# Projecting the next pair's K, Q and values inside the last norm of the pair before

## The reference, cut to what matters

```python
h = _L0_tok_ref(x, ...)                              # token mixing
h = _layernorm(h + _L0_attn_ref(h, ...), axis=-1)    # selective scan, norm 0
h = _layernorm(h + _L0_ffn_ref(h, ...), axis=-1)     # 16 experts, top 2, norm 1
h = _layernorm(h + _L1_attn_ref(h, ...), axis=-1)    # windowed attention, norm 2
h = _layernorm(h + _L1_ffn_ref(h, ...), axis=-1)     # routed two-layer FFN, norm 3

def _L0_tok_ref(x, d_gamma, Wq, bq, Wk, bk, Wv, bv, Wo, bo, prelu_a):
    q = x @ Wq + bq;  k = x @ Wk + bk;  v = x @ Wv + bv
    scores = jnp.einsum('btd,bsd->bts', q, k)
    retained = jnp.einsum('bts,bsd->btd', d_gamma * scores, v)
    y = retained @ Wo + bo
    return jnp.where(y >= 0, y, prelu_a * y)

def _layernorm(x, axis=-1, eps=1e-05):
    m = jnp.mean(x, axis=axis, keepdims=True);  v = jnp.var(x, axis=axis, keepdims=True)
    return (x - m) / jnp.sqrt(v + eps)
```

## Time and profile before

| | |
|---|---|
| median of three runs | 1545.95 us (1545.62 to 1551.45) |
| the profiled execution's own time | 1543.89 us |
| its span, first to last instruction | 1542.1 us |
| TensorE busy | 1319.3 us, 86% |
| VectorE busy | 1057.0 us, 69% |
| ScalarE busy | 603.4 us, 39% |
| GpSimd busy | 461.8 us, 30% |
| mean granted TensorE clock | 0.946 of full speed |

### The profile page before, as it was taken

How to read it: one execution, slowest core, us unless ns; L and a number is a source line. 1 busy time by engine, 2 the same in 40 slices (tenths; PEclk the granted TensorE clock), 3 DMA queues, 4 the chain that set the end, 5 groups by cost and what they waited for, 6 DMA issues and landing times. The chain is left out here.

```text
span 1542.1 us, 16298 instructions
## 1 busy us (share of the span) xinstructions
PE 1319.3 (86%) x5546; PEld 562.1 (36%) x5546; DVE 1057.0 (69%) x1218; ACT 603.4 (39%) x887; POOL 461.8 (30%) x262
## 2 busy tenths in 40 slices
PE   6957789988986789999897778999989686999897
PEld 2312333346422233325632323332663232333265
DVE  2599955674559995567456998656736599755673
ACT  0344343344254435325425343432441634343334
POOL 3268800022007970002100896000300189400030
PEclk9979999998997999999898799999989889999997
DMA  8334420000013432000001342200000234210000
GB/s 245 102 126 150 149 63 7 1 1 1 14 44 118 148 131 69 1 0 1 1 14 58 123 164 96 69 1 1 1 1 14 71 134 164 81 46 0 1 1 14
DMA packets 43378, 93.63 MB, mean 61 GB/s; under 512 B 6786, under 2 KB 23970, under 8 KB 42786
## 3 DMA queue, kind: packets, MB, share of 16 engines
q1 hardware_dynamic: 42690, 88.25, 17.6%
q10 hardware_dynamic: 608, 4.34, 0.9%
HBM read 87.84 MB, written 4.73 MB: 60 GB/s over the span
## 5 line engine op out<-in xcount | busy, mean ns | idle before, releaser
L443 POOL TENSOR_TENSOR scratch<-scratch 128x1024 f32<-128x1024 f32 x124 | 297.4, 2414 | 354.5 <-DVE scratch L1138 353.5
L593 PE MATMUL ps<-scratch,consts 128*128 128x512 f32 x512 | 257.3, 637 | 6.2 <-POOL scratch L443 6.2
L457 POOL TENSOR_TENSOR work<-work,rmax 128x512 f32<-128x512 f32 x64 | 67.4, 1053 | 621.8 <-DVE rmax L1285 621.8
L1138 DVE TENSOR_TENSOR_SCAN scratch<-ps,scratch 128x1024 f32<-128x1024 f32 x100 | 225.5, 2278 | 0.5
L911 ACT ACTIVATE ps<-steps,vec 128x1024 f32<-128x1024 f32 x128 | 143.0, 1117 | 208.9 <-DVE scratch L1138 206.8
L1187 DVE TENSOR_TENSOR scratch<-scratch,ps 128x1024 f32<-128x1024 f32 x108 | 131.9, 1221 | 118.2 <-PE ps L654 114.4
L571 PE MATMUL ps<-bc,pick 128*128 128x512 bf16 x256 | 83.9, 412 | 141.5 <-DVE scratch L1127 104.3
L957 ACT ACTIVATE scratch<-ps 128x1024 f32<-128x1024 f32 x108 | 108.8, 1022 | 175.6 <-PE ps L641 175.6
L593 PEld LDWEIGHTS ps<-scratch,consts 128*128 128x128 f32 x512 | 104.3, 206 | 125.9 <-issue 99.0
L641 PE MATMUL ps<-h_odd,w 64*128 64x512 f32 x512 | 140.9, 636 | 3.8 <-ACT scratch L957 3.8
L654 PE MATMUL ps<-scratch,w 64*128 64x512 f32 x512 | 134.9, 602 | 8.5 <-DVE scratch L1187 8.5
(11 more groups left out here) (197 smaller groups left out, 1666.2 us busy)
## 6 DMA issues: line engine op xcount, KB each, us to landing
scratch<-c_rows SPq DMA_DIRECT2D x128, 512.0 KB, 3.8
steps<-routed_table SPq DMA_DIRECT2D x128, 64.5 KB, 1.9
decayT<-in_decayT SPq DMA_DIRECT2D x8, 512.0 KB, 16.5
work<-in_table ACTq DMA_DIRECT2D x1, 2064.0 KB, 13.8
routed_table<-work SPq DMA_DIRECT2D x1, 2064.0 KB, 6.4
w<-in_w ACTq DMA_DIRECT2D x4, 512.0 KB, 20.9
out<-h_even SPq DMA_DIRECT2D x4, 512.0 KB, 2.6
bc<-in_x_next SPq DMA_DIRECT2D x3, 512.0 KB, 3.6
```

The costliest lines, as they stand in the source:

```text
L443: pool.tensor_tensor(hc_slot(k), hs_slot(k), c_slot(k), ALU.mult).then_inc(sem["hc_ready"], 1)
L593: m = mm(ps[:, 6 + c, :], ident, hc_slot(k)[:, c * CH:(c + 1) * CH], start=(n == 0), stop=(n == NS - 1))
L1138: dve.tensor_tensor_scan(hs_slot(k), banks(dA_bank(k)), dbu_slot(k), 0.0, ALU.mult, ALU.add).then_inc(sem["scanned"], 1)
```

## The change

TensorE projects K and Q of the next pair, a half at a time, inside norm 3: half 0 between the two halves of the output projection, half 1 between the variances of chunks 1 and 2. The values come behind the last variance. VectorE copies half 0 of K and Q in front of its first product, half 1 between products 1 and 2, and the values behind the last product; the Q copies go from ScalarE to VectorE. The values use banks 2 and 3, K's, after K is copied. Norm 3's variances use banks 6 and 7 twice, so the third and the fourth wait for the `rstd` of the first and the second. Scores of unit 1 now wait for the values' copies, and scores of unit 2 for `pair_done`. The first pair does the same projections in front of its own units.

```diff
-        VAR_BANKS = ((2, 3, 4, 5), (0, 1, 6, 7), (0, 1, 2, 3), (6, 7, 2, 3))
+        VAR_BANKS = ((2, 3, 4, 5), (0, 1, 6, 7), (0, 1, 2, 3), (6, 7, 6, 7))
...
@@ TensorE
+            def mix_kq(pair, c):
+                pe.wait_ge(sem["x_loaded"], at(pair, "x_loaded", 16))
+                if pair:
+                    pe.wait_ge(sem["l1_first"], at(pair - 1, "l1_first", c + 1))
+                    pe.wait_ge(sem["l1_second"], at(pair - 1, "l1_second", c + 1))
+                pe.matmul(ps[:, 2 + c, :], wk_bd[:, :], xT[:, c * CH:(c + 1) * CH], start=True, stop=True)\
+                    .then_inc(sem["k_ps"], 1)
+                pe.matmul(ps[:, c, :], wq_bd[:, :], xT[:, c * CH:(c + 1) * CH], start=True, stop=True)\
+                    .then_inc(sem["q_ps"], 1)
+
+            def mix_values(pair):
+                pe.wait_ge(fold_sb, 1)
+                pe.wait_ge(sem["k_tok_sb"], at(pair, "k_tok_sb", NC))
+                for t in range(NT):
+                    m = pe.matmul(ps[:, 2 + t // 4, (t % 4) * P:(t % 4 + 1) * P], xT[:, t * P:(t + 1) * P],
+                                  wvo_bd[:, :], start=True, stop=True)
+                    if t % 4 == 3:
+                        m.then_inc(sem["vw_ps"], 1)
...
                     for c in chunks:
+                        if k == 3 and c >= 2:
+                            pe.wait_ge(sem["rstd"], at(pair, "rstd", NN * k + c - 1))
                         pe.wait_ge(sem["squared"], at(pair, "squared", NN * k + c + 1))
...
-                pe.wait_ge(sem["x_loaded"], at(pair, "x_loaded", 16))
-                for c in range(NC):
-                    mm(ps[:, c, :], wq_bd[:, :], xT[:, c * CH:(c + 1) * CH], start=True, stop=True)\
-                        .then_inc(sem["q_ps"], 1)
-                pe.wait_ge(pair_done, pair + 1)
-                for c in range(NC):
-                    mm(ps[:, 2 + c, :], wk_bd[:, :], xT[:, c * CH:(c + 1) * CH], start=True, stop=True)\
-                        .then_inc(sem["k_ps"], 1)
-                pe.wait_ge(fold_sb, 1)
-                for t in range(NT):
-                    m = mm(ps[:, 6 + t // 4, (t % 4) * P:(t % 4 + 1) * P], xT[:, t * P:(t + 1) * P], wvo_bd[:, :],
-                           start=True, stop=True)
...
+                if pair == 0:
+                    for c in range(NC):
+                        mix_kq(0, c)
+                    mix_values(0)
...
+                    if n == 1:
+                        pe.wait_ge(sem["vw_sb"], at(pair, "vw_sb", 2))
                     if n == 2:
-                        pe.wait_ge(sem["vw_sb"], at(pair, "vw_sb", 2))
+                        pe.wait_ge(pair_done, pair + 1)
...
                     m.then_inc(sem["r_ready"], 1)
-                norm(3)
+                    if c == 0 and pair + 1 < PAIRS:
+                        mix_kq(pair + 1, 0)
+                norm(3, range(NN // NC))
+                if pair + 1 < PAIRS:
+                    mix_kq(pair + 1, 1)
+                norm(3, range(NN // NC, NN))
+                if pair + 1 < PAIRS:
+                    mix_values(pair + 1)
...
@@ ScalarE
-                for c in range(NC):
-                    act.wait_ge(sem["q_ps"], at(pair, "q_ps", c + 1))
-                    act.activation(q_tok[:, c * CH:(c + 1) * CH], ps[:, c, :], ACT.Identity, bias=v("bq"))\
-                       .then_inc(sem["q_sb"], 1)
...
@@ VectorE
+            def mix_kq(pair, c):
+                if pair:
+                    dve.wait_ge(sem["l1_first"], at(pair - 1, "l1_first", NC))
+                cols = slice(c * CH, (c + 1) * CH)
+                dve.wait_ge(sem["k_ps"], at(pair, "k_ps", c + 1))
+                dve.tensor_scalar(k_tok[:, cols], ps[:, 2 + c, :], v("bk"), None, ALU.add).then_inc(sem["k_tok_sb"], 1)
+                dve.wait_ge(sem["q_ps"], at(pair, "q_ps", c + 1))
+                dve.tensor_scalar(q_tok[:, cols], ps[:, c, :], v("bq"), None, ALU.add).then_inc(sem["q_sb"], 1)
...
-                norm(3)
+                if pair + 1 < PAIRS:
+                    mix_kq(pair + 1, 0)
+                norm(3, range(NN // NC))
+                if pair + 1 < PAIRS:
+                    mix_kq(pair + 1, 1)
+                norm(3, range(NN // NC, NN))
+                if pair + 1 < PAIRS:
+                    mix_values(pair + 1)
                 dve.memset(m1[:, :], 0.0).then_inc(pair_done, 1)
```

More of the change, by code:

```diff
@@ L482, in norm @@
                             .then_inc(sem["var_ps"], 1)
-                pe.wait_ge(sem["x_loaded"], at(pair, "x_loaded", 16))
-                for c in range(NC):
-                    mm(ps[:, c, :], wq_bd[:, :], xT[:, c * CH:(c + 1) * CH], start=True, stop=True)\
-                        .then_inc(sem["q_ps"], 1)
-                pe.wait_ge(pair_done, pair + 1)
-                for c in range(NC):
-                    mm(ps[:, 2 + c, :], wk_bd[:, :], xT[:, c * CH:(c + 1) * CH], start=True, stop=True)\
-                        .then_inc(sem["k_ps"], 1)
-                pe.wait_ge(fold_sb, 1)
-                for t in range(NT):
-                    m = mm(ps[:, 6 + t // 4, (t % 4) * P:(t % 4 + 1) * P], xT[:, t * P:(t + 1) * P], wvo_bd[:, :],
-                           start=True, stop=True)
-                    if t % 4 == 3:
-                        m.then_inc(sem["vw_ps"], 1)
+                if pair == 0:
+                    for c in range(NC):
+                        mix_kq(0, c)
+                    mix_values(0)
                 def scores(n):
@@ L519, in _ @@
                         scores(n + 2)
+                    if n == 0:
+                        pe.wait_ge(pair_done, pair + 1)
                     pe.wait_ge(sem["masked"], at(pair, "masked", n + 1))
@@ L1037, in _, with mix_values @@
             dve.tensor_scalar(skip[:, :], ident, v("D"), None, ALU.mult).then_inc(skip_ready, 1)
+            def mix_kq(pair, c):
[6 more added lines that the diff above has]
+                dve.tensor_scalar(q_tok[:, cols], ps[:, c, :], v("bq"), None, ALU.add).then_inc(sem["q_sb"], 1)
+            def mix_values(pair):
+                for c in range(2):
+                    dve.wait_ge(sem["vw_ps"], at(pair, "vw_ps", c + 1))
+                    dve.tensor_tensor(vw[:, 4 * c:4 * c + 4, :], ps[:, 2 + c, :].rearrange("p (a b) -> p a b", a=4),
+                                      vo_row[:, :].unsqueeze(1).to_broadcast([P, 4, P]), ALU.add)\
+                       .then_inc(sem["vw_sb"], 1)
             for pair in range(PAIRS):
```

## The result

The changed kernel is slower: 1557.4 us median (1555.95 to 1560.78) against 1547.3 (1545.62 to 1551.45) for the kernel before in the same comparison, ratio 1.0064 with a 95% interval of 1.0037 to 1.0092, about 10 us. That is 0.4 us above the upper end of the predicted range, and above the bound of 0.5% inside which it was forecast.

The account below looks back on a forecast made before the run. TensorE was taken to bound each boundary, with 0.60 us to win. Three boundaries (3.75) plus the last norm (1.8) added 5.55 us to the median 1545.95, giving 1551.5; range 1546 to 1557, the forecast's own 1548 to 1553.5.

Parts of the forecast that it names:

- What bounds a boundary, TensorE with 0.60 us to win: Between pairs, TensorE was said to set the length, busy 9.28 of 9.88 us, with 0.60 us idle to win.
- The chain through the norm: From foT through norm 3 to the next pair's retained matmul: each boundary 1.25 us longer, bounds 0.8 to 1.7.
- The wait on `rstd`, put together as 0.78: Norm 3's third and fourth variances: an Ln starts 0.78 us after an Exp has ended, bounds 0.51 and 1.2.
- First half of K and Q: Between the two foT halves: its matmuls gain nothing by themselves and delay the norm by 1.81 us.
- Q on VectorE: Q's copies at the boundary, moved from ScalarE to VectorE: no cost forecast for the move alone.
- the start of pair 0: K before Q in the first pair: costed at nothing, covered by the fifth mask's 3.35 us wait for the decay transfer.
- The clock in the boundary: TensorE's granted clock between pairs was forecast to stay 1.00 through the new idle of about 1.15 and 0.83 us.
- the third rival: At boundaries the clock falls to half rate, losing some 6 us each: 1569.5, or 1560 if back sooner; chance 0.07.
- The base: Whole kernel before: a median of 1545.95 us, to which the forecast's sum was added.
- the sum of 5.55: Whole kernel: 3.75 us for three boundaries plus 1.8 for the last pair's norm, other parts costed at nothing.
- From there TensorE is busy without a gap to 438, so nothing gives the loss back: Behind the first retained matmul after a boundary: TensorE has no gap, so the boundary's 1.25 us loss stays.
- The second rival: Slow engine hand-offs, 0.31 us each, in the boundary chain: 2.75 a boundary, 2.6 at the end, 1557; chance 0.14.

Follow-up runs that it names:

- e4: Kernel before, with K of the next pair waiting for the third rstd of the last norm instead of `pair_done`; 1555.93 us, 1.0045.
- e10: Kernel before with only norm 3's banks (6, 7, 6, 7) and the two rstd waits, nothing projected early; 1.0073.
- e11: Changed kernel with the first half of K and Q moved behind variances 0 and 1, in front of the second half; 1.0057 to the kernel before.
- e12: Kernel before with only Q's two copies moved from ScalarE to VectorE, each behind K's copy of the same half; 0.9977.
- e2: Kernel before with two chained VectorE memsets in front of the one that raises `pair_done`, delaying K at each boundary; 1560.84 us, 1.0093.
- e3: Kernel before with four chained VectorE memsets in front of the one that raises `pair_done`; 1574.85 us, 1.0177.
- e1: The changed kernel run once more, unaltered; 1556.57 us, 1.0071 to the kernel before.
- e5: Kernel before with two more 512-column matmuls between K and the values of pairs 1 to 3; 1.0052.
- e8: Kernel before with one more 512-column matmul between K and the values of pairs 1 to 3; 1.0020.
- e6: Kernel before with four more 512-column matmuls between K and the values of pairs 1 to 3; 1.0064.
- e13: Kernel before with six idle-filling matmuls per pair in the tail of the attention; 1543.11 us, 0.9963.

## Why the prediction was wrong

*What bounds a boundary, TensorE with 0.60 us to win:* right. e4 takes that wait away and gets 0.86: the 0.60, and 0.26 of TensorE's busy time (12.05 to 11.79).

*The chain through the norm:* right in each link, and off by a little. The third square came 4.05 after L826 started (forecast 3.79), Ln 2 at 7.25 (6.99), product 1 at 8.06 (7.82), the values at 9.35 (9.10), the scores at 11.30 (10.98), the first mask at 12.55 (12.23), the retained matmul at 14.17 (13.75 to 14.1). The 0.25 that all carry was lost in front of the third square: I gave the joints between foT, K and Q no time of their own. TensorE's two stops were shorter than forecast (0.87 and 0.57 for 1.15 and 0.83), but its busy time, for which the chain had no term, grew by 0.68. A boundary cost 1.52 where I took 1.25 (bounds 0.8 to 1.7).

*The wait on `rstd`, put together as 0.78:* Exp 0 of the last pair ends at 1551.87 and Ln 2 starts at 1552.66, 0.79. Ln 3 is 6.21 after foT, as worked out, and the end grew by 1.76 (1.8). e10 confirms the same price at a boundary.

*First half of K and Q, "they delay the norm by 1.81":* the squares moved, but it is not what the boundary paid for; e11 puts it at 0.36.

*Q on VectorE, the start of pair 0:* Q 0.26 in e12, forecast nothing alone. At the start the values came 0.06 earlier (18.04 before, 17.98 after) and the first mask 0.02 later, so nothing was lost there by the order; but the start itself varies by 3 us from one execution to another (58.05 to 61.34 in the table, in no order of the kernels).

*The clock in the boundary:* right, 1.00, and the third rival did not come true there. e2 and e3 show how far it was away: behind a wait of 4.35 us the next two matmuls ran at half rate in e3, behind three equal waits of 2.48 in e2 only the last time (3.54, and 1.98 twice). The Trainium skill (TensorE: Matmul & The Clock Gate, section "HAM oscillation — how this bites in real kernels") says that idle gaps between bursts send the array to half rate, and the next burst pays. The row of K in e3 agrees with it, and e2's rows agree in one of three.

*The base:* the kernel before came out at 1547.3 beside the change and not at 1545.95, so 1.35 of the 5.9 us between forecast and measurement is no part of the change. On the forecast's own base the measured 10.1 would have given 1556.1, inside the range; on which side of the range's end the time fell is luck. The other 4.5 are what the sum lacks.

*The step that failed* is the sum of 5.55. It counts three boundaries and an end, and puts the stages between, some 337 us a pair from the first convolution matmul to foT, at nothing. The sentence that stands for it, "From there TensorE is busy without a gap to 438, so nothing gives the loss back", holds for the 29 us that it names (29.61 from the retained matmul to the convolution in pairs 1 to 3 of every trace) and says nothing of what follows. The local part measures 6.3 and would have been in the range. What the sum lacks is in the pairs: 7.5 us more in the first trace of the change and 6.4 in e1's, by two long pairs of 340.5 in each, which stand against none among the last three pairs in both traces of the kernel before. A long pair differs from a short one by VectorE's product beside GpSimd's (2.75 for 0.67) and by where the low-clock stretches lie. The earlier trace rows shows the low clock behind the attention, and I read it as a property of a place. The single stretches in the scan, which I did not look at, move when a boundary moves. That long pairs are no mark of this change, e4, e5 and e8 show: shorter or longer boundaries, with no early projection at all, have them too.

The second rival named 1557, the time that came, but not by its mechanism: the hand-offs are not slow (0.79 for the trip), and a boundary cost 1.52 and not 2.75.

*What stays open.* Which shift brings long pairs and which doesn't: none of the runs gives a rule, and the one I tried (e6) failed. No run changed the order of VectorE's product and L451 alone, so what the product costs by itself is read from traces and not tested, and why it takes 2.75 beside L451 no run shows. The 6.3 us are shown to be the change's, by place and size, in every trace of it. How much of the rest is the change's isn't shown: half of the kernel before's own times are above 1551, none of those executions was traced, and beside the later medians of 1550.6 to 1551.8 the change was not run again (6.3 over them would be 1557 to 1558, about where it was measured). The interval of the first measurement (6 to 14 us) would hold 6.3 alone, that of e1 (7 to 15) just not.

## What to carry to other kernels

Before moving work into an idle engine's gap, ask which engine sets the length of that stretch: here TensorE was busy 9.28 of 9.88 us, so the best outcome was 0.6 us, and PSUM banks saved at the price of two return trips through another engine cost three times that. Where the clock of TensorE changes level in the stages behind, or an operation's length depends on what another engine does beside it, a shift of a microsecond can cost or give several there, so judge a change of under 1% by the stretches of both traces, boundary by boundary, and not by the total alone, and trace a long execution of the kernel before as well as a short one. And a stage whose matmuls are small and wait for each other may be worth filling: six idle matmuls a pair won 0.4%, and with a shorter boundary 1.2%.

## What the runs showed of the hardware that was not expected

Removing 0.86 us from each of three boundaries made a kernel 7 us slower (e4), and the same removal on top of e13 made it 9 to 13 us faster. From the first convolution to foT the same instructions took from 335.8 to 342.3 us in traces without e13's matmuls, in stages that differ by where the granted clock was low and by one product of VectorE; the 29.6 us in front of them repeat to 0.01 us. That product took 0.67 us ahead of GpSimd's L451 and 2.75 when it started 0.15 behind it, in 28 and 40 pairs with nothing between. And a stretch at the low clock isn't always a loss: the pairs that had one 116 us behind their first convolution matmul were the short ones.
